# Patch stage of a vision tower: images loaded by channel into 112 partitions, half images in groups of 16, four result buffers

## The chip, the cores and the metric

The kernel runs on one core of one Trainium2 chip. The metric is the device time of one execution, in microseconds. Three executions of the kernel before gave 3536.22, 3531.46 and 3524.28 us, so the median is 3531.46 us.

## What is computed

64 images of 3 x 224 x 224 are cut into patches of 16 x 16 and turned into 64 x 196 tokens of 192 numbers; an attention layer and a feed-forward layer with a mixture of four experts follow. Only the first part bears on the change:

```python
B, c, H, Wd = features.shape            # 64, 3, 224, 224
h, w = (H // P1, Wd // P2)              # 14 x 14 patches
x = features.reshape(B, c, h, P1, w, P2)
x = jnp.transpose(x, (0, 2, 4, 3, 5, 1))
x = x.reshape(B, h * w, P1 * P2 * c)    # 768 numbers a patch
x = _layernorm(x, ln1_g, ln1_b)
x = jnp.einsum('bnd,de->bne', x, W) + b # 768 -> 192
x = _layernorm(x, ln2_g, ln2_b)
```

Everything after it (two attention phases named a and b, and the feed-forward phase f) reads these tokens from device memory and is the same in both kernels.

## The kernel before

The program runs four phases one after the other: tokenize_phase, attention_phase twice, ffn_phase. At the end of each phase all engines meet, so the next phase starts when the slowest engine of the phase is done; SP waits there for its last stores. All tiles of the patch stage bear the prefix t_ in the profile.

**Tiling.** A group is 8 whole images. One row of patches of one image is one partition, so a group fills 8 x 14 = 112 partitions (R), and each partition holds 3 channels x 3584 numbers (16 pixel lines of 224), in t_rows. There are two such buffers. A group is worked off in 7 units (UPG) of two patch columns each, so 8 groups make 56 units (NU). A unit u goes through four steps, each on several engines:

- A: DVE takes statistics of the two columns (L1036, L1043), POOL makes of them a scale and a shift (L27, L29, L952, L954);
- B: ACT applies these (t_xn, L990), PE transposes the result (L1082), ACT rounds it to 16 bits (t_xh, L995), DVE takes the rest (t_xl, L1049);
- C: PE multiplies with the weights in three passes (t_yp, L776; 38 matmuls a unit with the bias), DVE takes the statistics of the result (L1056, L1060), POOL makes scale and shift (L27, L29, L967, L969);
- D: ACT applies them (t_yn, L1005), POOL multiplies and adds the second affine pair (L958, L960), SP stores the tokens (L921).

**Order.** Each engine runs the same function `step` for s = -2 ... 56, and in step s it works on A of unit s+2, B of s+1, C of s and D of s-1. An engine executes what its step lists in that order and stops at each semaphore that isn't there yet. POOL's step lists A, D, C. The middle steps are a loop in the program (Fori, L869) of 14 steps a round; the first steps and the last ones are written out.

**Loads and stores.** SP issues all of them, in one queue. The next group's 8 images are loaded one by one, 588 KB each, two images in each of the first four units of a group, into the buffer that the group before has left (L903). A unit's tokens are stored as 112 rows of 384 numbers, 168 KB (L921). In SP's step the two loads stand ahead of the store. t_yn has two buffers: ACT may write unit u into its buffer when the store of unit u-2 has landed, and SP waits with the store of unit u-1 until the one before has landed:

```python
wait(act, out_s, 16 * (u - 1))          # ACT, ahead of L1005
waits(sp, (aff, 2 * (s - 1) + 2), (out_s, 16 * (s - 1)))   # SP, ahead of L921
```

At the start SP first issues 21 small loads (weights, L893; gains and offsets, L896; rows that are copied to all partitions, L898), and then the first group's 8 images.

Of the kernel before, what the change touches and what calls it, by code (L numbers as in the profile page):

```python
# [779 lines left out]
def tokenize_phase(nc, img, dst, ln1_g, ln1_b, w, bias, ln2_g, ln2_b):  # L780
# [19 lines left out]
    with ExitStack() as ctx:  # L800
        def sb(label, shape, dt):
            return ctx.enter_context(nc.sbuf_tensor(f"t_{label}", shape, dt))
# [41 lines left out]
        eps2 = sb("eps2", [R, 2], F32)  # L844
        yn = [sb(f"yn{i}", [R, 2, dim], F32) for i in range(2)]

# [3 lines left out]
        consts, w_in, w_ok, bp_s = sem("consts"), sem("w_in"), sem("w_ok"), sem("bp_s")  # L850
        rows_in = sem("rows_in")
# [3 lines left out]
        aff, out_s = sem("aff"), sem("out_s")  # L855

        LAG = {"A": 2, "B": 1, "C": 0, "D": -1}
        BODY = 2 * UPG

        def steps(eng, body):  # L860

            def kinds(s):
                return {k for k, lag in LAG.items() if 0 <= s + lag < NU}
            first = 3
            n = (NU - 2 - first) // BODY
            for s in range(-2, first):
                body(s, s, 0, kinds(s))
            if n > 0:
                with eng.Fori(0, n) as i:  # L869
                    for c in range(first, first + BODY):  # L870
                        body(BODY * i + c, c, i, set(LAG))
            for s in range(first + BODY * max(n, 0), NU + 1):
                body(s, s, 0, kinds(s))

        def group(c, i, lag):

            g, v = divmod(c + lag, UPG)
            return 2 * i + g, g % 2, v

# [3 lines left out]

        out_rows = dst.rearrange("(r x) d -> r x d", x=cols)
        block = ctx.enter_context(nc.Block())

        @block.sync
        def _(sp):
            w_view = w.rearrange("(q c) e -> c q e", c=chans)
            per = feats // chans // 128  # L890
            for k in range(KT):
                c, q = divmod(k, per)
                sp.dma_start(wraw[:, k, :], w_view[c, q * 128:(q + 1) * 128, :]).then_inc(w_in, 16)  # L893
                for col, vec in ((gcol, ln1_g), (bcol, ln1_b)):
                    v = vec.rearrange("(q c) -> c q", c=chans)[c, q * 128:(q + 1) * 128].rearrange("(p o) -> p o", o=1)
                    sp.dma_start(col[:, k:k + 1], v, allow_slow_non_contiguous=True).then_inc(w_in, 16)  # L896
# [27 lines left out]
            steps(sp, step)  # L924
            sp.wait_ge(out_s, 16 * NU)

        @block.gpsimd
        def _(pool):
# [15 lines left out]

            def step(s, c, i, kinds):
                if "A" in kinds:
                    u, b = s + 2, c % 2
# [7 lines left out]
                if "D" in kinds:  # L955
                    u, b = s - 1, (c - 1) % 2
                    wait(pool, yn_s, 2 * (u + 1))
                    pool.tensor_tensor(yn[b][:], yn[b][:], g2[:].unsqueeze(1).to_broadcast([R, 2, dim]), ALU.mult).then_inc(aff, 1)  # L958
                    wait(pool, aff, 2 * u + 1)
                    pool.tensor_tensor(yn[b][:], yn[b][:], b2[:].unsqueeze(1).to_broadcast([R, 2, dim]), ALU.add).then_inc(aff, 1)  # L960
                if "C" in kinds:
                    u, b = s, c % 2
# [8 lines left out]
            steps(pool, step)  # L971

        @block.scalar
        def _(act):
            act.wait_ge(w_in, 16 * (3 * KT + 3))
            act.mul(g16[:], gcol[:], WSCALE).then_inc(w_ok, 1)
# [5 lines left out]

            def step(s, c, i, kinds):
                if "B" in kinds:
                    u, b = s + 1, (c + 1) % 2
                    _, gb, v = group(c, i, 1)
                    for t in range(2):
# [9 lines left out]
                if "D" in kinds:  # L997
                    normalise(s - 1, (c - 1) % 2)

            def normalise(u, b):  # L1000

                wait(act, sh2_s, 2 * (u + 1))
                wait(act, out_s, 16 * (u - 1))
                for t in range(2):
                    act.activation(yn[b][:, t, :], yp[b][0:R, t * dim:(t + 1) * dim], ACT.Identity,  # L1005
                                   scale=rstd2[b][:, t:t + 1], bias=shift2[b][:, t:t + 1]).then_inc(yn_s, 1)

            steps(act, step)

        @block.vector  # L1010
        def _(dve):
# [14 lines left out]

            def step(s, c, i, kinds):
                if "A" in kinds:
                    u, b = s + 2, c % 2
                    g, gb, v = group(c, i, 2)  # L1030
                    wait(dve, rows_in, 16 * G_IMG * (g + 1))
                    wait(dve, mv_s, 2 * u)
# [4 lines left out]
                if "A" in kinds:  # L1037
                    u, b = s + 2, c % 2
                    wait(dve, sh_s, 2 * (u - 1))
# [4 lines left out]
                if "B" in kinds:  # L1044
                    u, b = s + 1, (c + 1) % 2
                    for t in range(2):
# [4 lines left out]
                if "C" in kinds:  # L1051
                    u, b = s, c % 2
                    wait(dve, yp_s, u + 1)
# [7 lines left out]

            steps(dve, step)

        @block.tensor
        def _(pe):
# [7 lines left out]

            def step(s, c, i, kinds):
                if "B" in kinds:
# [8 lines left out]
                if "C" in kinds:  # L1084
                    u, b = s, c % 2
                    for t in range(2):
# [7 lines left out]

            steps(pe, step)

# [919 lines left out]
```

## Time and profile before

| what | us |
|---|---|
| median of the three runs | 3531.46 |
| the profiled execution, its own time | 3541.15 |
| its span in the trace | 3539.1 |
| patch stage: from the start to the first instruction of the next phase | 523.84 |
| first instruction on an image's data | 63.39 |

The profiled execution is 9.7 us above the median and 2.05 us longer than its span. PE is busy for 84% of the whole span, DVE for 68%, ACT for 52%, POOL for 42%; in the patch stage the shares are lower. A row of the profile names the line, the engine, the operation and the tiles. In brackets stands the idle time of the engine ahead of it and what ended that time. SPq is SP's queue of transfers. The DMA share is the mean busy share of the core's 16 DMA engines.

### The profile page before, as it was taken

How to read it: one execution, taken by the hardware profiler on the slowest of the kernel's cores; microseconds unless marked ns; L12 is line 12 of the kernel's file. 1: busy time of each engine (PE TensorE's matmuls, PEld its weight loads, DVE VectorE, ACT ScalarE, POOL GpSimd, SP SyncE). 2: the span in 40 equal slices, each digit the busy share in tenths (PEclk: the TensorE clock that was granted, in tenths of full speed). 3: DMA queues.
4: the chain of work that ended last, by engine and by line, in shares of the span. 5: the costliest groups of instructions: out<-in, count | busy, mean ns of one | idle time of the engine just before them, and what ended most of it. 6: DMA issues, size and time to landing. Idle time of an engine off the chain costs nothing. (4 is left out here: it accounts for less than half of the span.)

```text
span 3539.1 us, 96114 instructions
## 1 busy us (share of the span) xinstructions
PE 2979.8 (84%) x31553; PEld 2278.1 (64%) x31553; DVE 2417.1 (68%) x5681; ACT 1849.0 (52%) x3603; POOL 1487.5 (42%) x2221
## 2 busy tenths in 40 slices
PE   2676766999999994899999997689987599999998
PEld 2666654556556652455556554678886488888887
DVE  2564656788888863788888884565555577777776
ACT  2454553666666661566666664556654244444443
POOL 1555562233333313344444431246666444444444
PEclk9887886999999996799999998899998799999999
DMA  7777733555555542465666653444433344444443
GB/s 93 103 105 100 106 59 89 133 140 148 145 138 143 141 123 68 121 157 149 154 154 160 156 150 91 124 117 131 124 120 103 92 66 66 66 65 66 66 66 50
DMA packets 503782, 393.69 MB, mean 111 GB/s; under 512 B 219818, under 2 KB 485068, under 8 KB 500812
## 3 DMA queue, kind: packets, MB, share of 16 engines
q1 hardware_dynamic: 465004, 343.59, 42.6%
q0 software_dynamic: 38496, 46.38, 7.5%
q8 instruction: 172, 2.82, 0.4%
q14 instruction: 110, 0.90, 0.1%
HBM read 232.59 MB, written 155.42 MB: 110 GB/s over the span
## 5 line engine op out<-in xcount | busy, mean ns | idle before, releaser
L1455 POOL DMA_INDIRECT out_dram<-f_yo,f_idg x202 | 331.5, 1641 | 426.7 <-DVE f_yo L1789 393.2
L566 DVE TENSOR_REDUCE b_mx<-b_mxp 98x4 f32<-98x784 f32 x384 | 371.5, 967 | 142.0 <-PE b_mxp L705 137.5
L566 DVE TENSOR_REDUCE a_mx<-a_mxp 98x4 f32<-98x784 f32 x384 | 371.5, 967 | 135.4 <-PE a_mxp L705 131.0
L1529 ACT ACTIVATE f_hf<-f_bank,f_b1c 128x256 f32<-128x256 f32 x606 | 254.3, 473 | 236.4 <-PE f_bank L776 236.3
L465 ACT ACTIVATE b_pt<-b_st 98x784 f32<-98x784 f32 x384 | 315.1, 821 | 61.0 <-PE b_st L691 57.5
L465 ACT ACTIVATE a_pt<-a_st 98x784 f32<-98x784 f32 x384 | 315.1, 821 | 58.7 <-PE a_st L691 55.4
L1945 PE MATMUL f_bank<-f_w2h,f_hh 128*128 x1212 | 299.7, 247 | 23.9 <-DVE f_hl L1773 23.4
L1946 PE MATMUL f_bank<-f_w2h,f_hl 128*128 x1212 | 298.2, 246 | 0.0
L1947 PE MATMUL f_bank<-f_w2l,f_hh 128*128 x1212 | 298.2, 246 | 0.0
L1082 PE MATMUL t_turned<-t_ident,t_xn 112*128 112x112 f32 x672 | 104.9, 313 | 179.0 <-ACT t_xn L990 174.3
L776 PE MATMUL f_bank<-f_el,f_w1h 128*128 128x256 f16 x1212 | 232.4, 274 | 0.0
L421 POOL TENSOR_TENSOR a_cn<-a_ctxs,a_rec 128x392 f32<-128x392 f32 x96 | 95.3, 1021 | 316.4 <-DMA a_rec<-a_recip 316.4
L1576 DVE TENSOR_TENSOR f_hl<-f_hf,f_hh 128x512 f16<-128x512 f32 x147 | 100.9, 686 | 184.9 <-ACT f_hf L1486 182.8
L1428 POOL DMA_INDIRECT f_listed<-f_xr,f_idx x196 | 200.7, 1024 | 57.1 <-issue 54.3
L1773 DVE TENSOR_TENSOR f_hl<-f_hf,f_hh 128x512 f16<-128x512 f32 x303 | 209.9, 693 | 10.4
L1082 PEld LDWEIGHTS t_turned<-t_ident,t_xn 112*128 112x128 f32 x672 | 84.3, 169 | 195.2 <-ACT t_xn L990 138.2
L766 PE MATMUL b_pr<-b_pf,b_cn 128*98 128x192 f32 x768 | 190.3, 359 | 23.1 <-DVE b_xo L613 16.0
L421 POOL TENSOR_TENSOR b_cn<-b_ctxs,b_rec 128x392 f32<-128x392 f32 x96 | 95.3, 1022 | 267.9 <-DMA b_rec<-b_recip 267.9
L766 PE MATMUL a_pr<-a_pf,a_cn 128*98 128x192 f32 x768 | 187.1, 354 | 23.6 <-DVE a_xo L613 16.0
L1521 ACT ACTIVATE f_xf<-f_bank,f_bcol,f_gcol 128x256 f32<-128x256 f32 x202 | 103.2, 561 | 179.5 <-PE f_bank L1915 179.5
L776 PE MATMUL t_yp<-t_wh,t_xh 128*112 128x192 f16 x672 | 182.6, 272 | 0.0
L776 PE MATMUL t_yp<-t_wl,t_xh 128*112 128x192 f16 x672 | 181.3, 270 | 0.0
(372 smaller groups left out, 9263.4 us busy)
## 6 DMA issues: line engine op xcount, KB each, us to landing
t_rows<-in_x_dram SPq DMA_DIRECT2D x64, 588.0 KB
f_xg<-f_listed SPq DMA_DIRECT2D x101, 264.0 KB, 2.8
a_qk<-a_qkh SPq DMA_DIRECT2D x128, 147.0 KB, 2.9
a_rec<-a_recip SPq DMA_DIRECT2D x128, 147.0 KB, 3.4
b_qk<-b_qkh SPq DMA_DIRECT2D x128, 147.0 KB, 2.8
b_rec<-b_recip SPq DMA_DIRECT2D x128, 147.0 KB, 3.5
a_qst<-a_qk SPq DMA_DIRECT2D x128, 110.2 KB, 3.0
a_kst<-a_qk SPq DMA_DIRECT2D x128, 110.2 KB, 3.1
```

The costliest lines, as they stand in the source:

```text
L421: pool.tensor_tensor(cn[b][:, g, :], ctxs[b][:, g, :], rec[:, g, :], ALU.mult).then_inc(cn_s, 1)
L465: act.activation(pt[k % PT][:].rearrange("p j a t -> p j (a t)"), st_ps[0:half_t, :, 0:unit_t], ACT.Exp, scale=sm_scale).then_inc(exp_s, 1)
L566: dve.tensor_reduce(mx[:, a, :, 2 * p:2 * p + 2].rearrange("p q j -> p j q"), mx_ps[0:half_t, :, 0:unit_t].rearrange("p j (q t) -> p j q t ...
L766: ins = pe.matmul(pr_ps[0:half_t, 0:dim], cn[b][:, g, x * half_t:(x + 1) * half_t], pf[:, g, :], start=(g == 0), stop=(g == 2))
L776: ins = pe.matmul(out, lhs, rhs, start=(i == 0), stop=(i == len(terms) - 1))
L1428: pool.indirect_dma_start(listed, bass.IndirectOffsetOnAxis(ap=idx[b % 2][:, 2 * (u - first_unit[b]) + t, c:c + 1], axis=0), xr[:, 2 * (u ...
L1455: pool.indirect_dma_start(out, bass.IndirectOffsetOnAxis(ap=idg[i % 3][:, t:t + 1], axis=0), yo[i % 3][:, t, :], None, compute_op=ALU.add) ...
L1529: act.activation(hf[pair][:, c % 2, :], p1[q % 2][:, (c % 2) * T:(c % 2) * T + T], ACT.Gelu, bias=b1c[:, bass.ds(e, 1), c], scale=1.0 / WS ...
L1773: dve.tensor_tensor(hl[i % 2][:, cs, :], hf[pair][:], hh[i % 2][:, cs, :], ALU.subtract).then_inc(ehl_s, 1)
L1945: pe.matmul(o, hh[i % 2][:, j, ts], high, start=(j == 0), stop=False)
L1946: pe.matmul(o, hl[i % 2][:, j, ts], high, start=False, stop=False)
L1947: pe.matmul(o, hh[i % 2][:, j, ts], low, start=False, stop=False)
```

## The change

Only the patch stage is changed.

1. A group is half of 16 images: 7 patch rows of each, again 112 partitions, 7 units and 56 units in all. The two halves of the same 16 images follow each other.
2. The load of a group is three transfers (N_LOADS), one for each channel, each into all 112 partitions, 14,336 bytes in each. One is issued in each of the first three units of a group. The two t_rows buffers have a semaphore each.
3. The first group's three loads are issued by ACT, at its very start, not by SP behind the weights.
4. The gains and offsets come in 6 transfers, not 12, so SP issues 15 small loads at the start, not 21.
5. t_yn has four buffers with a semaphore each. ACT waits for the store of unit u-4, and SP no longer waits for a store ahead of a store.
6. On SP, the store of a step stands ahead of the load. On POOL, the step lists A, C, D.
7. The loop is gone: all steps are written out on every engine.

```diff
-    G_IMG = 8
-    R = G_IMG * cols
-    n_groups = n_img // G_IMG
+    G_IMG = 16
+    G_ROWS = cols // 2
+    R = G_IMG * G_ROWS
+    n_groups = 2 * n_img // G_IMG
+    PARTS = 1
+    N_LOADS = chans * PARTS
+    YN = 4
...
-        yn = [sb(f"yn{i}", [R, 2, dim], F32) for i in range(2)]
+        yn = [sb(f"yn{i}", [R, 2, dim], F32) for i in range(YN)]
...
+        def load(eng, g, which):
+            c, part = divmod(which, PARTS)
+            src = img[g // 2 * G_IMG:(g // 2 + 1) * G_IMG, c].rearrange("i (h l) x -> i h l x", l=patch)
+            src = src[:, g % 2 * G_ROWS:(g % 2 + 1) * G_ROWS, part * lines:(part + 1) * lines].rearrange("i h l x -> i h (l x)")
+            to = rows[g % 2][:, c, part * lines * side:(part + 1) * lines * side]
+            eng.dma_start(to, src).then_inc(rows_in[g % 2], 16)
...
-            def load(g, b, images):
-                for j in images:
-                    src = img[bass.ds(g * G_IMG + j, 1)].rearrange("o c (h l) x -> (o h) c (l x)", l=patch)
-                    sp.dma_start(rows[b][j * cols:(j + 1) * cols], src).then_inc(rows_in, 16)
-
-            def step(s, c, i, kinds):
+            def step(s, kinds):
+                if "D" in kinds:
+                    u = s - 1
+                    g, v = divmod(u, UPG)
+                    wait(sp, aff, 2 * (u + 1))
+                    to = out_rows[g // 2 * G_IMG:(g // 2 + 1) * G_IMG, g % 2 * G_ROWS:(g % 2 + 1) * G_ROWS, 2 * v:2 * v + 2]
+                    sp.dma_start(to.rearrange("i h x d -> i h (x d)"),
+                                 yn[u % YN][:].rearrange("r x d -> r (x d)")).then_inc(out_s[u % YN], 16)
                 if "B" in kinds:
-                    g, gb, v = group(c, i, 1)
-                    if v < G_IMG // 2 and not (isinstance(g, int) and g + 1 >= n_groups):
+                    u = s + 1
+                    g, v = divmod(u, UPG)
+                    if v < 3 and g + 1 < n_groups:
                         if v == 0:
-                            waits(sp,
-                                  (xn_s, 2 * (s + 1)),
-                                  (st_s, 4 * (s + 1) + 1))
-                        else:
-                            wait(sp, xn_s, 2 * (s + 1))
-                        load(g + 1, 1 - gb, (2 * v, 2 * v + 1))
-                if "D" in kinds:
-                    g, gb, v = group(c, i, -1)
-                    waits(sp,
-                          (aff, 2 * (s - 1) + 2),
-                          (out_s, 16 * (s - 1)))
-                    sp.dma_start(out_rows[bass.ds(g * R, R), 2 * v:2 * v + 2, :], yn[(c - 1) % 2][:]).then_inc(out_s, 16)
-
-            load(0, 0, range(G_IMG))
+                            wait(sp, xn_s, 2 * u)
+                            wait(sp, st_s, 4 * u)
+                        for which in range(v * N_LOADS // 3, (v + 1) * N_LOADS // 3):
+                            load(sp, g + 1, which)
...
         def _(act):
-            act.wait_ge(w_in, 16 * (3 * KT + 3))
+            for which in range(N_LOADS):
+                load(act, 0, which)
+            act.wait_ge(w_in, 16 * (KT + 2 * chans + 3))
...
                 wait(act, sh2_s, 2 * (u + 1))
-                wait(act, out_s, 16 * (u - 1))
+                wait(act, out_s[u % YN], 16 * (u // YN))
```

**POOL, two units in the middle of the stage.** t_rstd and t_shift are step A's, the ones with _0 and _1 step C's, t_yn is step D's. Before:

```order
L27 TENSOR_TENSOR t_rstd<-t_mv,t_eps 112x2 [waits t_xn_s,t_mv_s]
L29 TENSOR_TENSOR t_rstd<-t_rstd,t_minus_half 112x2 [waits t_rsqrt_s]
L952 TENSOR_TENSOR t_shift<-t_mv,t_rstd 112x2 [waits t_rsqrt_s]
L954 TENSOR_TENSOR t_shift<-t_shift,t_minus_one 112x2 [waits t_sh_s]
L958 TENSOR_TENSOR t_yn<-t_yn,t_g 112x384 [waits t_yn_s]
L960 TENSOR_TENSOR t_yn<-t_yn,t_b 112x384 [waits t_aff]
L27 TENSOR_TENSOR t_rstd_0<-t_mv_0,t_eps 112x2 [waits t_yn_s,t_mv2_s]
L29 TENSOR_TENSOR t_rstd_0<-t_rstd_0,t_minus_half 112x2 [waits t_rsqrt2_s]
L967 TENSOR_TENSOR t_shift_0<-t_mv_0,t_rstd_0 112x2 [waits t_rsqrt2_s]
L969 TENSOR_TENSOR t_shift_0<-t_shift_0,t_minus_one 112x2 [waits t_sh2_s]
```

The two long operations on t_yn stand between A and C. In the changed kernel, in the same place:

```order
L27 TENSOR_TENSOR t_rstd<-t_mv,t_eps 112x2 [waits t_xn_s,t_mv_s]
L29 TENSOR_TENSOR t_rstd<-t_rstd,t_minus_half 112x2 [waits t_rsqrt_s]
L944 TENSOR_TENSOR t_shift<-t_mv,t_rstd 112x2 [waits t_rsqrt_s]
L946 TENSOR_TENSOR t_shift<-t_shift,t_minus_one 112x2 [waits t_sh_s]
L27 TENSOR_TENSOR t_rstd_0<-t_mv_0,t_eps 112x2 [waits t_yn_s,t_mv2_s]
L29 TENSOR_TENSOR t_rstd_0<-t_rstd_0,t_minus_half 112x2 [waits t_rsqrt2_s]
L953 TENSOR_TENSOR t_shift_0<-t_mv_0,t_rstd_0 112x2 [waits t_rsqrt2_s]
L955 TENSOR_TENSOR t_shift_0<-t_shift_0,t_minus_one 112x2 [waits t_sh2_s]
L959 TENSOR_TENSOR t_yn<-t_yn,t_g 112x384 [waits t_yn_s]
L961 TENSOR_TENSOR t_yn<-t_yn,t_b 112x384 [waits t_aff]
```

C now follows A directly, and the two operations on t_yn stand between C and the next unit's A.

**SP, around a group's first load.** Before (in the loop; the ISA rows hold waits on registers):

```order
L921 ISA [waits t_out_s,t_aff]
L921 DMA tokens<-t_yn 112x384
L39 ISA
L903 ISA [waits t_st_s,t_xn_s]
L903 DMA t_rows<-in_x_dram 14x3x3584
L903 ISA
L903 DMA t_rows<-in_x_dram 14x3x3584
```

In the changed kernel (x5 and the like: so many of the same in a row):

```order
L903 DMA tokens<-t_yn 16x7x384 [waits t_aff] x5
L879 DMA t_rows<-in_x_dram 112x1x3584 [waits t_st_s,t_xn_s]
L903 DMA tokens<-t_yn 16x7x384 [waits t_aff]
L879 DMA t_rows<-in_x_dram 112x1x3584
L903 DMA tokens<-t_yn 16x7x384 [waits t_aff]
L879 DMA t_rows<-in_x_dram 112x1x3584
L903 DMA tokens<-t_yn 16x7x384 [waits t_aff] x5
```

A store waits for POOL's result alone, and eight loads of 14 partitions have become three of 112.

**ACT, at the start of the program.** In the changed kernel the first group's loads stand ahead of all else there (before, ACT's first row is the one on t_g):

```order
L879 DMA t_rows<-in_x_dram 112x1x3584 x3
L970 ACT_TABLE_LOAD
L970 ACTIVATE t_g<-t_gcol 128x6 [waits t_w_in]
L974 ACTIVATE t_wf<-t_wraw,t_g 128x192 [waits t_consts,t_w_ok]
```

## Rows read from the trace of the kernel before

**Rows 1.** Waits between 161.7 and 219.9: engine, line, releaser, total, times, longest.

```profile
ACT t_yn L1005 <- DMA tokens<-t_yn: 28.0, 5, 6.8
POOL t_yn L958 <- ACT t_yn L1005: 19.8, 4, 6.7
```

**Rows 2.** SP's queue over one group, start and length in us.

```profile
161.68 18.91 SPq L921 DMA_DIRECT2D tokens<-t_yn  x4
...
208.34 0.35 SPq L921 DMA_DIRECT2D tokens<-t_yn  x1
208.98 0.84 SPq L903 DMA_DIRECT2D t_rows<-in_x_dram  x2
219.94 0.35 SPq L921 DMA_DIRECT2D tokens<-t_yn  x1
```

**Rows 3.** Stretches: PE, PEld, DVE, ACT, POOL busy, granted clock, DMA share, GB/s.

```profile
208.30:219.90 11.60, 7.42 (x50) 7.23 (x50) 3.97 (x12) 4.18 (x7) 4.53 (x10) 0.69 0.90 119
161.70:219.90 58.20, 40.25 (x350) 38.03 (x350) 32.62 (x100) 29.30 (x43) 31.54 (x70) 0.85 0.73 102
478.00:508.00 30.00, 25.41 (x267) 23.05 (x266) 24.12 (x78) 23.83 (x34) 25.52 (x57) 1.00 0.10 30
524.00:528.00 4.00, 0.00 (x0) 0.00 (x0) 3.29 (x2) 0.00 (x0) 1.39 (x9) 0.50 0.79 154
1904.00:1908.00 4.00, 3.77 (x43) 2.47 (x45) 2.45 (x4) 1.67 (x4) 0.00 (x0) 1.00 0.71 174
```

**Rows 4.** Start of the program, in order of time.

```profile
10.73 63.60 SPq L903 DMA_DIRECT2D t_rows<-in_x_dram  x14
15.55 0.21 ACT L976 ACTIVATE t_g<-t_gcol 128x6 f32<-128x6 f32 x1 [13.46 <-DMA t_b<-in_L_tok_ln_b_dram]
...
24.89 0.42 DVE L1024 SCALAR_TENSOR_TENSOR t_brow_parts<-t_brow_hi,t_row_mask,t_brow 112x192 f16<-112x192 f16 x1
63.39 1.94 DVE L1036 BATCH_NORM_STATS2 t_stats<-t_rows 112x6 f32<-112x384 f32 x4 [38.08 <-DMA t_rows<-in_x_dram]
```

**Rows 5.** Order of time without loads, one unit's path from 482.08.

```profile
482.08 0.20 POOL L27 TENSOR_TENSOR t_rstd<-t_mv,t_eps 112x2 f32<-112x2 f32 x1
...
483.64 1.95 ACT L990 ACTIVATE t_xn<-t_rows,t_shift,t_rstd 112x768 f32<-112x768 f32 x2 [0.56 <-POOL t_shift L954]
...
489.33 0.25 PE L776 MATMUL t_yp<-t_brow_parts,t_first_two 112*112 112x192 f16 x1
...
490.38 0.15 DVE L1060 BATCH_NORM_AGGREGATE t_mv<-t_stats 112x2 f32<-112x6 f32 x1
...
491.37 0.19 POOL L27 TENSOR_TENSOR t_rstd<-t_mv,t_eps 112x2 f32<-112x2 f32 x1
...
492.85 0.20 POOL L27 TENSOR_TENSOR t_rstd<-t_mv,t_eps 112x2 f32<-112x2 f32 x1
...
494.40 1.95 ACT L990 ACTIVATE t_xn<-t_rows,t_shift,t_rstd 112x768 f32<-112x768 f32 x2 [0.56 <-POOL t_shift L954]
```

**Rows 6.** PE in the first unit (slow clock) and later, in order of time.

```profile
74.98 0.37 PE L776 MATMUL t_yp<-t_wh,t_xh 128*112 128x192 f16 x1
...
75.14 0.37 PE L776 MATMUL t_yp<-t_wl,t_xh 128*112 128x192 f16 x1
...
80.62 0.25 PE L776 MATMUL t_yp<-t_wh,t_xh 128*112 128x192 f16 x1
...
80.71 0.25 PE L776 MATMUL t_yp<-t_wl,t_xh 128*112 128x192 f16 x1
```

**Rows 7.** First and last units on ACT and POOL, and the next phase's first instruction.

```profile
81.47 0.92 ACT L1005 ACTIVATE t_yn<-t_yp,t_shift,t_rstd 112x192 f32<-112x192 f32 x2 [0.63 <-POOL t_shift L969]
...
513.68 0.91 ACT L1005 ACTIVATE t_yn<-t_yp,t_shift,t_rstd 112x192 f32<-112x192 f32 x2 [4.07 <-DMA tokens<-t_yn]
518.25 0.91 ACT L1005 ACTIVATE t_yn<-t_yp,t_shift,t_rstd 112x192 f32<-112x192 f32 x2 [3.66 <-POOL t_shift L969]
...
523.84 0.74 POOL L364 MEMSET a_praw<- 96x768 f32 x1 [2.53 <-POOLq L800]
```

More of the change, by code:

```diff
@@ L850, in tokenize_phase @@
         consts, w_in, w_ok, bp_s = sem("consts"), sem("w_in"), sem("w_ok"), sem("bp_s")
-        rows_in = sem("rows_in")
+        rows_in = [sem(f"rows_in{i}") for i in range(2)]
         st_s, mv_s, rsqrt_s, sh_s = sem("st_s"), sem("mv_s"), sem("rsqrt_s"), sem("sh_s")
@@ L854, in tokenize_phase, with steps @@
         yp_s, sh2_s, st2_s, mv2_s, rsqrt2_s, yn_s = (sem("yp_s"), sem("sh2_s"), sem("st2_s"), sem("mv2_s"), sem("rsqrt2_s"), sem("yn_s"))
-        aff, out_s = sem("aff"), sem("out_s")
+        aff, out_s = sem("aff"), [sem(f"out_s{i}") for i in range(YN)]
         LAG = {"A": 2, "B": 1, "C": 0, "D": -1}
[L858 to L878, printed above, removed]
+        def steps(body):
+            for s in range(-2, NU + 1):
+                body(s, {k for k, lag in LAG.items() if 0 <= s + lag < NU})
         def patches(buf, col):
             return buf[:].rearrange("r c (l x) -> r (c l) x", l=patch)[:, :, col * patch:(col + 1) * patch]
-        out_rows = dst.rearrange("(r x) d -> r x d", x=cols)
+        out_rows = dst.rearrange("(i h x) d -> i h x d", h=cols, x=cols)
+        lines = patch // PARTS
+        def load(eng, g, which):
[4 more added lines that the diff above has]
+            eng.dma_start(to, src).then_inc(rows_in[g % 2], 16)
         block = ctx.enter_context(nc.Block())
@@ L893, in _ @@
                 sp.dma_start(wraw[:, k, :], w_view[c, q * 128:(q + 1) * 128, :]).then_inc(w_in, 16)
-                for col, vec in ((gcol, ln1_g), (bcol, ln1_b)):
-                    v = vec.rearrange("(q c) -> c q", c=chans)[c, q * 128:(q + 1) * 128].rearrange("(p o) -> p o", o=1)
-                    sp.dma_start(col[:, k:k + 1], v, allow_slow_non_contiguous=True).then_inc(w_in, 16)
+            for col, vec in ((gcol, ln1_g), (bcol, ln1_b)):
+                for c in range(chans):
+                    v = vec.rearrange("(q p c) -> c p q", c=chans, p=128)[c]
+                    sp.dma_start(col[:, c * per:(c + 1) * per], v, allow_slow_non_contiguous=True).then_inc(w_in, 16)
@@ L927, in _ @@
+                        for which in range(v * N_LOADS // 3, (v + 1) * N_LOADS // 3):
+                            load(sp, g + 1, which)
+            steps(step)
+            for i in range(YN):
+                sp.wait_ge(out_s[i], 16 * ((NU - i + YN - 1) // YN))
         @block.gpsimd
@@ L943, in _, with step @@
                                pattern=[[-1, 128]], channel_multiplier=1).then_inc(consts, 1)
-            def step(s, c, i, kinds):
+            def step(s, kinds):
                 if "A" in kinds:
-                    u, b = s + 2, c % 2
+                    u, b = s + 2, s % 2
                     wait(pool, mv_s, 2 * (u + 1))
@@ L969, in step @@
                     pool.tensor_tensor(shift2[b][:], shift2[b][:], minus_one[:], ALU.mult).then_inc(sh2_s, 1)
-            steps(pool, step)
+                if "D" in kinds:
+                    u, b = s - 1, (s - 1) % YN
+                    wait(pool, yn_s, 2 * (u + 1))
+                    pool.tensor_tensor(yn[b][:], yn[b][:], g2[:].unsqueeze(1).to_broadcast([R, 2, dim]), ALU.mult).then_inc(aff, 1)
+                    wait(pool, aff, 2 * u + 1)
+                    pool.tensor_tensor(yn[b][:], yn[b][:], b2[:].unsqueeze(1).to_broadcast([R, 2, dim]), ALU.add).then_inc(aff, 1)
+            steps(step)
         @block.scalar
         def _(act):
-            act.wait_ge(w_in, 16 * (3 * KT + 3))
+            for which in range(N_LOADS):
+                load(act, 0, which)
+            act.wait_ge(w_in, 16 * (KT + 2 * chans + 3))
             act.mul(g16[:], gcol[:], WSCALE).then_inc(w_ok, 1)
@@ L981, in _, with step @@
                 act.mul(bspread[:, k, :], ones[:], bcol[:, k:k + 1]).then_inc(w_ok, 1)
-            def step(s, c, i, kinds):
+            def step(s, kinds):
                 if "B" in kinds:
-                    u, b = s + 1, (c + 1) % 2
-                    _, gb, v = group(c, i, 1)
+                    u, b = s + 1, (s + 1) % 2
+                    g, v = divmod(u, UPG)
+                    gb = g % 2
                     for t in range(2):
@@ L1025, in _, with step @@
                                      op0=ALU.mult, op1=ALU.add).then_inc(bp_s, 1)
-            def step(s, c, i, kinds):
+            def step(s, kinds):
                 if "A" in kinds:
-                    u, b = s + 2, c % 2
-                    g, gb, v = group(c, i, 2)
-                    wait(dve, rows_in, 16 * G_IMG * (g + 1))
+                    u, b = s + 2, s % 2
+                    g, v = divmod(u, UPG)
+                    gb = g % 2
+                    wait(dve, rows_in[gb], 16 * N_LOADS * (g // 2 + 1))
                     wait(dve, mv_s, 2 * u)
@@ L1060, in step @@
                         dve.bn_aggr(mv2[b][:, t, :], stats2[:, t, :]).then_inc(mv2_s, 1)
-            steps(dve, step)
+            steps(step)
         @block.tensor
@@ L1072, in _, with step @@
             pe.wait_ge(w_ok, 3 + 2 * KT)
-            def step(s, c, i, kinds):
+            def step(s, kinds):
                 if "B" in kinds:
@@ L1084, in step @@
                 if "C" in kinds:
-                    u, b = s, c % 2
+                    u, b = s, s % 2
                     for t in range(2):
@@ L1093, in step @@
                     ins.then_inc(yp_s, 1)
-            steps(pe, step)
+            steps(step)
 def ffn_phase(nc, x3, h1, out, mlp, experts, ln_g, ln_b, gate_w, gate_b):
```

22 lines of the change are left out of this document (7 added, 15 removed).

## The prediction

> **What bounds the kernel now.** Only the patch stage changes, so I read the profile by stage: it ends at 523.84 us [rows 7], and what follows keeps its instructions and its time. In the stage three views matter. The waits over one group [rows 1] say who ends last: ACT waits 28.0 of 58.2 us for the store of the tokens before it may write t_yn, and POOL's 19.8 us of waiting for t_yn is the same wait passed on. SP's queue [rows 2] says why: four units without loads between their stores go by in 18.9 us, 6.3 us a step, while a unit whose two images were just queued takes 11.6 us (208.34 to 219.94). Two images are 2 x 602,112 bytes, so loads move at 1.204 MB / 11.6 us = 103.8 GB/s, and the store sits behind them in the queue; with the store's 172,032 bytes that makes the 119 GB/s of the stretch [rows 3]. So the images' transfer sets the step there, through the store and the two t_yn buffers. Second, the start: nothing touches an image before 63.39 us, because 8 images have to land first [rows 4]. Third, the order of time where no load is under way [rows 5] shows what is left if transfers are hidden: two units in 494.40 - 483.64 = 10.76 us, 5.38 us each.
>
> The DMA share tells how the loads are slow. It is 0.90 in that stretch, close to 14 engines of 16, and 119 GB/s over 0.90 x 16 engines is 8 GB/s for each busy engine. In 478 to 508, where nearly all traffic is stores from 112 partitions, 30 GB/s take a share of 0.10, or 300 GB/s at a full share; loads of weights into 96 and 128 partitions give 154 / 0.79 = 195 and 174 / 0.71 = 245 [rows 3]. An engine can do more than these loads get out of it.
>
> **Part 1, load rate (item 2).** A new load is 112 x 14,336 bytes = 1.606 MB. No row shows one of this shape. Bounds: 103.8 GB/s (15.5 us) from the loads it replaces, 300 GB/s (5.4 us) from the stores. I take 245 GB/s, 6.6 us, the value of the nearest full-width load. What does it have to meet? SP issues a group's first load behind the store of the unit u-2 (u is the group's first), that is when POOL begins A of unit u+2. The next group's first statistics must be done when POOL begins A of u+7: five steps, 30 us at the step found below, less 2.3 us for the statistics themselves. In it lie three loads, five stores at 172,032 B / 300 GB/s = 0.57 us, and some 2 us of latency: (30 - 2.3 - 2.9 - 2.1) / 3 = 7.6 us a load, 211 GB/s. At 245 the loads are hidden; at 195 (8.2 us) each of 7 groups waits 3 x 0.6 = 1.9 us, 13 us in all, which goes into the range.
>
> The Trainium skill ("SBUF — State Buffer", section on the DMA port swizzle) says that four adjacent partitions share one of 16 ports of some 27 GB/s. By that, 14 adjacent partitions have 4 on one port, 172 KB, an estimated 6.3 us or 95 GB/s an image, near the 5.8 us measured; and 112 partitions have at most 8 on a port, 115 KB, an estimated 4.2 us a load. The sum would be the same by it, since such a load is hidden as well.
>
> **Part 2, four t_yn buffers, no store behind store (item 5).** ACT now has two more steps for a store to land. A store behind one load is late by 6.6 us plus its own 2 or 3, far under the three steps it has; the 28.0 us go. I cost the rest at nothing, with the loads as cover as above.
>
> **Part 3, POOL's order (item 6).** Something else is late next. Take unit u's A on POOL, ended at 483.61 (1.53 us from 482.08), and follow [rows 5]: t_xn from 483.64, transposes, then the products of the unit before, the last at 489.33 + 0.25 = 489.58; its statistics are there at 490.53. Before, POOL is then still in D until 491.4, takes C (491.37 to 492.85, 1.5 us), and A of unit u+2 from 492.85 to 494.37. The loop spans two steps, 10.76 us. Three of POOL's pieces fill 482.08 to some 487.1, so D is 2.06 us. In the changed order C starts at once at 490.6, but D comes between C and that A: 483.61 to 490.6 is 7.0, + 1.5 + 2.06 + 1.5 = 12.06 us for two steps, **6.0 us a unit** against 5.38. POOL's own work is 5.1 us a unit, PE's 25.41 us of 30 at a step of 5.38, so 4.6 us; DVE 4.3, ACT 4.3 [rows 3]: none is the bound. The reorder is thus paid in this loop, 0.64 us a unit, though the step still falls from 8.3 (58.2 / 7).
>
> **Part 4, the start (items 3 and 4).** The statistics of unit 0 stand on DVE behind the work on the weights, which ended 9.8 us after the small loads were in (15.55 to 25.31) [rows 4]. The images come beside the weights now. If the weights are not disturbed: 25.3 us. If they land last of 4.82 + 0.84 MB at 245 GB/s: 0.8 + 23.1 + 9.8 = 34 us; at 195, 40 us. SP's queue is done six issues earlier. I take 30.
>
> **Part 5, the rest.** Written-out steps: nothing on the path; the last 13 units were written out before as well and include the 5.38 us stretch. From the first statistics to the first t_yn it took 81.47 - 63.39 = 18.1 us, kept. The last interval is 4.6 us (513.68 to 518.25). Behind the last t_yn came 5.6 us (518.25 to 523.84) [rows 7]; now D of unit 54 is still on POOL then, 1.1 more: 6.7.
>
> **Sum.** 30 + 18.1 + 54 x 6.0 + 4.6 + 6.7 = 383.4 us instead of 523.8, **140.4 us less**. 3541.15 - 140.4 = 3400.7 for a profiled execution; that lay 9.7 above the median, so **3391 us**, 4.0% less.
>
> **Rivals.**
>
> A. *POOL's order does not bind* (its pieces shift so that the old step holds): 54 x 0.62 = 33.5 us less, 3357. For it: POOL has idle time. Against it: the loop above has no slack in it.
>
> B. *The PE clock drops.* In the loaded group the granted clock was 0.85, in 478 to 508 it was 1.00 [rows 3]; a matmul starts every 0.16 us at the low level and every 0.08 at the high one [rows 6], so 38 of them cost 3.0 us more per loop, 1.5 us a unit if always slow (+81 us). At 0.85, some 0.3 of it: +24, 3415; half slow: +40, 3431. Against it: the long waits of PE, after which it was slow, go with the store waits, and the new step has gaps of about 1.4 us.
>
> C. *An engine gets no more out of a load than before* (slower). If what holds the loads is the rate of a DMA engine on rows of 14,336 bytes, then 16 engines instead of 14 give 103.8 x 16 / 14 = 118.6 GB/s, 13.5 us a load. Each group then takes 42 + 3 x (13.5 - 7.6) = 60 us; the start waits for 5.7 MB, about 55 us. 55 + 7 x 60 + 18.1 + 30 + 4.6 + 6.7 = 534 us, 10 more than before, and up to 25 more where the second group's loads share the start: some 3550 us. For it: the share of 0.90 means 14 busy engines. Against it: the rates of rows 3. It decides from about 120 GB/s down; above that the kernel is faster. The Trainium skill ("DMA: Bandwidth & Descriptors", section on the semaphore increment by 16) has a transfer run on the largest number of engines up to 16 that divides the slowest dimension of both sides: 14 before, which the trace agrees with, and 16 now.
>
> D. *A load does not spread at all*: its source has 16 images of 7 rows, its target 112 partitions. If it fell on 7 engines or fewer at the 300 / 16 = 19 GB/s of a store's engine, it would run at 130 GB/s or less: no gain, and with one engine a multiple of the stage.
>
> **How the numbers follow.** Forecast 0.74, A 0.08, B 0.08, C 0.07, D 0.03. The forecast's own range: start 25 to 40 (-5, +10), loads at 195 (+13), step 5.9 to 6.2 (-5, +11): 3380 to 3425. The range takes in A and B up to half slow and leaves out C and D: 3350 to 3440. A measurement can tell 0.3% (11 us) from no change. Faster by more: 0.91; within: 0.03 (part of C and D); slower: 0.06.
>
> **What would show it.** Right: first statistics near 30 us; no wait of ACT for the store; DVE's waits for t_rows near nothing after the first; t_yn every 6.0 us; POOL's step A of u+2 starting straight behind D while its statistics are already there; a granted clock near 1.0; the stage over at 383. A DMA share near 1 with long DVE waits for t_rows would mean C; a step of 5.4 means A; a clock of 0.85 or less with a step of 6.5 or more means B. Wrong: a stage end under 345 or over 435 us.

## The result

The changed kernel took 3400.99 us at the median of four runs (3387.60 to 3413.05), the kernel before 3527.87 us in the runs beside it (3524.12 to 3536.22). The ratio is 0.9636, with a 95% interval of 0.9595 to 0.9678: 3.6% less time. 3391 us were forecast, in a range of 3350 to 3440. The profiled execution took 3402.21 us. Six later runs of the same code (below, e12) lay higher, at a median of 3424.60 us and a ratio of 0.9706 (0.966 to 0.9751), so the changed kernel scatters more than the one before (those six lie 46 us apart, eleven of the kernel before beside them 31 us).

### The profile page after: what moved, and what is told of

Its sections match the earlier page's. It is cut to its first block and busy times, and to the rows that moved or that the text cites. A ratio compares the mean times of both kernels' runs of the same rounds, so it can differ in the third digit from the quotient of the medians.

```text
span 3400.3 us, 95327 instructions
## 1 busy us (share of the span) xinstructions
PE 2948.0 (87%) x31553; PEld 2234.3 (66%) x31553; DVE 2409.6 (71%) x5681; ACT 1847.6 (54%) x3603; POOL 1485.2 (44%) x2221
## 3 DMA queue, kind: packets, MB, share of 16 engines
q10 hardware_dynamic: 384, 4.82, 0.5%
## 5 line engine op out<-in xcount | busy, mean ns | idle before, releaser
L720 PE MATMUL b_pv<-b_pt,b_vp 98*32 98x196 f32 x3072 | 172.2, 342 | 0.2 <-ACT b_mrow L492 0.2
L720 PE MATMUL a_pv<-a_pt,a_vp 98*32 98x196 f32 x3072 | 169.8, 339 | 0.1
L776 PE MATMUL f_bank<-f_eh,f_w1h 128*128 128x256 f16 x606 | 165.6, 273 | 3.5 <-DVE f_el L1759 3.5
L776 PE MATMUL t_yp<-t_wh,t_xh 128*112 128x192 f16 x672 | 166.3, 247 | 0.0
```

The lines of the kernel that those rows point to most:

```text
L720: ins = pe.matmul(pv_ps[32 * h4:32 * h4 + 32, 0:tok], vp[b][:, 2 * a + kt, h, :], pt[(first + h4) // 2 % PT][:, h4 % 2, kt, :], start=(kt ...
L776: ins = pe.matmul(out, lhs, rhs, start=(i == 0), stop=(i == len(terms) - 1))
```

## The profile after

The span of the profiled execution, and the end of the stage on SP's queue (start, length): the last run of stores, then the next phase's first load.

```profile
span 3400.3 us, 95327 instructions
```

```profile
321.85 66.23 SPq L903 DMA_DIRECT2D tokens<-t_yn  x13
390.51 0.36 SPq L250 DMA_DIRECT2D a_wraw<-in_L_attn_w_qkv_dram  x1
```

The stage now ends at 390.5 us, 133.3 us earlier than the 523.84 of [rows 7]. The spans differ by 138.8; the other 5.5 us lie behind the stage, where both kernels have the same instructions. That part took 3015.3 us before and 3009.8 after, and between 2990 and 3020 us in all the profiles of this case, so I count it as scatter.

The longest of the waits between 60 and 330 us (engine and line, who released it, total us, times, longest us), which answer to [rows 1]:

```profile
PEld t_turned L1078 <- ACT t_xn L985: 74.8, 89, 1.6
ACT t_xn L985 <- POOL t_shift L946: 74.0, 45, 1.9
DVE t_stats L1052 <- PE t_yp L776: 60.3, 45, 1.5
PE t_turned L1078 <- ACT t_xn L985: 51.0, 44, 1.4
POOL t_rstd L27 <- DVE t_mv L1056: 43.4, 44, 1.2
ACT t_xh L990 <- PE t_turned L1078: 9.0, 45, 0.2
```

No DMA stands among them, nor among the shorter ones: ACT waits for no store and DVE for no image. What is left is one ring of short waits, a unit at a time: POOL for DVE's statistics of the product, ACT for POOL, PE for ACT, DVE for PE. It is the loop that the forecast named.

Stretches of the trace (busy us and instructions of PE, PEld, DVE, ACT, POOL, then granted clock, DMA share, GB/s), which answer to [rows 3]:

```profile
136.00:152.00 16.00, 12.35 (x130) 11.13 (x129) 11.99 (x41) 11.49 (x16) 11.35 (x28) 1.00 0.99 258
61.00:374.00 313.00, 246.15 (x2603) 225.05 (x2602) 231.53 (x725) 216.80 (x313) 233.25 (x521) 1.00 0.47 128
```

While a group's three loads run one behind the other, the engines move 258 GB/s at a share of 0.99, where 119 GB/s at 0.90 stood before, and over 313 us the granted clock stays at 1.00.

The step, on ACT and POOL (start, length, in brackets the idle time before it), which answers to [rows 5]:

```profile
205.23 1.00 POOL L959 TENSOR_TENSOR t_yn<-t_yn,t_g 112x384 f32<-112x384 f32 x1
206.31 1.00 POOL L961 TENSOR_TENSOR t_yn<-t_yn,t_b 112x384 f32<-112x384 f32 x1
207.26 0.20 POOL L27 TENSOR_TENSOR t_rstd<-t_mv,t_eps 112x2 f32<-112x2 f32 x1
...
208.83 1.95 ACT L985 ACTIVATE t_xn<-t_rows,t_shift,t_rstd 112x768 f32<-112x768 f32 x2 [1.46 <-POOL t_shift L946]
...
220.86 1.95 ACT L985 ACTIVATE t_xn<-t_rows,t_shift,t_rstd 112x768 f32<-112x768 f32 x2 [1.45 <-POOL t_shift L946]
```

POOL starts A at 207.26, straight behind the two operations of D, while its statistics were ready at 205.9 (DVE, L1039). Two units take 220.86 - 208.83 = 12.03 us, 6.0 us each.

The start, which answers to [rows 4]:

```profile
0.81 2.03 ACTq L879 DMA_DIRECT2D t_rows<-in_x_dram  x3
...
5.73 12.93 SPq L893 DMA_DIRECT2D t_bcol<-in_L_tok_ln_b_dram  x3
...
27.79 0.21 ACT L970 ACTIVATE t_g<-t_gcol 128x6 f32<-128x6 f32 x1 [23.64 <-DMA t_b<-in_L_tok_ln_b_dram]
...
37.12 1.93 DVE L1032 BATCH_NORM_STATS2 t_stats<-t_rows 112x6 f32<-112x384 f32 x4
```

The first statistics come at 37.12 us instead of 63.39, and they wait for the work on the weights and no longer for an image.

## Experiments

Each kernel is the changed one with the edit named. Ratios are to the kernel before, run beside it.

### What brings the gain: the loads or the buffers

**e2: the old loads, four buffers.**

```diff
-    G_IMG = 16
-    G_ROWS = cols // 2
+    G_IMG = 8
+    G_ROWS = cols
...
-    N_LOADS = chans * PARTS
+    N_LOADS = G_IMG
...
+            j = g * G_IMG + which
+            src = img[j:j + 1].rearrange("o c (h l) x -> (o h) c (l x)", l=patch)
+            to = rows[g % 2][which * cols:(which + 1) * cols]
...
-                    if v < 3 and g + 1 < n_groups:
+                    if v < 4 and g + 1 < n_groups:
```

Two images are issued in each of a group's first four units, and the store's rows follow the new groups.

> The changed kernel with the old loads alone: groups of 8 whole images, one load of 14 partitions for each image, two in each of the first four units; four t_yn buffers, no store waiting for a store, and all else as changed. Theory (the rate of the loads is what counts; the store waits were only where it showed): a group needs 4.82 MB at 104 GB/s = 46.4 us in a window of 27.7 us, so it takes 42 + 24 = 66 us, DVE waits for t_rows some 24 us a group, ACT for no store, and the time is some 3590 us, 1.017 of before. Rival (the store waits were the cause, and four buffers cure them with slow loads too): steps of 6 us, near 3420 us.

Measured: 3582.40 us, ratio 1.0166 (1.0129 to 1.0203). DVE's waits between 60 and 330 us, the first statistics of two groups in a row, and between them the issue of the second group's first images:

```profile
DVE t_stats L1031 <- DMA t_rows<-in_x_dram: 78.4, 4, 22.9
```

```profile
117.84 1.94 DVE L1031 BATCH_NORM_STATS2 t_stats<-t_rows 112x6 f32<-112x384 f32 x4 [11.91 <-DMA t_rows<-in_x_dram]
...
134.91 0.79 SPq L878 DMA_DIRECT2D t_rows<-in_x_dram  x2
...
184.71 1.94 DVE L1031 BATCH_NORM_STATS2 t_stats<-t_rows 112x6 f32<-112x384 f32 x4 [21.98 <-DMA t_rows<-in_x_dram]
```

A group takes 184.71 - 117.84 = 66.9 us and the next 64.9, against the 66 worked out, and no wait of ACT for a store is left. The theory holds: the wait that stood on top before, ACT for the store, can be removed altogether, and the kernel becomes slower, because the images still come slowly (4.82 MB in the 49.8 us from 134.91 to 184.71, 97 GB/s) and DVE waits for them instead. It is slower than the kernel before because the rest of the change costs something where loads are slow. In the kernel before, SP issued the next group's first images 9.2 us behind a group's first statistics (114.27 and 123.42 us in its trace), here 17.1 us behind them (117.84 and 134.91). These 8 us are what a group takes more than the 58.2 us of before. The likely reasons are the new order on SP, where the load now stands behind the store, and the new order on POOL, which makes that store later; no run tests them.

**e4: the old loads, two buffers** (e2 with `YN = 2`).

> The changed kernel with the old loads (8 images of 14 partitions a group) and two t_yn buffers, the rest as changed. The kernel with the old loads and four buffers took 3582 us. Theory (with slow loads the buffers don't matter either: a group waits for its images, and a store wait only falls into that wait): 3580 to 3600 us. Rival (four buffers were worth something with slow loads): over 3620 us.

Measured: 3584.40 us, ratio 1.0148 (1.0113 to 1.0183). ACT's wait for the store is back, and DVE's wait for images is smaller, 50.7 us in place of 78.4, in the same 270 us:

```profile
ACT t_yn L999 <- DMA tokens<-t_yn: 76.8, 13, 7.3
DVE t_stats L1031 <- DMA t_rows<-in_x_dram: 50.7, 4, 12.9
```

3582 and 3584 us: with slow loads the number of buffers makes no difference that this can measure. ACT's 76.8 us of waits cost nothing, because a group ends with its images either way.

**e3: the new loads, two buffers** (`YN = 2`).

> The changed kernel with two t_yn buffers, nothing else. Theory (with fast loads the buffers matter little): a store lands 2.5 us after issue and 7.1 behind a load; with two buffers ACT is held up to 2.3 us three times a group, of which 1.5 us are slack, so 0 to 20 us more than the changed kernel: 3400 to 3420 us, 0.964 to 0.970 of before. Rival (the buffers are an equal part of the gain): ACT waits for stores as before, over 60 us more, over 0.98 of before.

Measured: 3424.50 us (3397.24 to 3438.04), ratio 0.970 (0.9639 to 0.9762), just above what the theory gave. But the trace does not show the mechanism that I expected. Between 60 and 330 us ACT waited once for a store, in the 17th of its steps:

```profile
ACT t_yn L1000 <- DMA tokens<-t_yn: 1.3, 1, 1.3
```

```profile
164.72 0.91 ACT L1000 ACTIVATE t_yn<-t_yp,t_shift,t_rstd 112x192 f32<-112x192 f32 x2 [1.28 <-DMA tokens<-t_yn]
```

Yet the stage ended at 434.33 us, 43.8 later than with four buffers, and the step was 6.83 us from the third unit to the end. A row of PE, a stretch of two steps and one of 50 us (columns as in [rows 3], the granted clock third from the end):

```profile
209.65 1.72 PE L1078 MATMUL t_turned<-t_ident,t_xn 112*128 112x112 f32 x12 [2.86 <-ACT t_xn L985]
```

```profile
204.00:206.00 2.00, 2.00 (x27) 2.00 (x26) 1.87 (x7) 1.36 (x3) 1.83 (x4) 1.00 0.99 301
206.00:208.00 2.00, 0.79 (x10) 0.59 (x8) 1.96 (x8) 0.00 (x0) 1.84 (x3) 1.00 0.57 159
208.00:210.00 2.00, 0.35 (x4) 0.35 (x5) 1.86 (x6) 1.43 (x2) 1.62 (x7) 1.00 0.52 136
210.00:212.00 2.00, 1.88 (x18) 1.67 (x17) 1.00 (x4) 1.80 (x3) 1.92 (x4) 0.84 0.99 251
212.00:214.00 2.00, 2.00 (x15) 2.00 (x14) 0.95 (x2) 1.39 (x4) 1.28 (x5) 0.50 0.95 258
...
100.00:150.00 50.00, 40.59 (x377) 39.16 (x378) 31.76 (x99) 31.77 (x46) 31.41 (x72) 0.86 0.52 141
```

Two steps run close together, then PE waits 2.86 us for ACT, and about 2 us after it has started again its clock stands at 0.50 (1.2 GHz) for some 3 us. A matmul then starts every 0.16 us, not every 0.08, the products are late, and with them the next pair of steps: the pattern makes the gap that keeps it alive. In the changed kernel, with four buffers, PE's two gaps were 1.35 and 0.97 us and the clock stayed at 1.00.

How it began stands 100 us ahead of the only wait for a store:

```profile
59.30 1.71 PE L1078 MATMUL t_turned<-t_ident,t_xn 112*128 112x112 f32 x12 [1.60 <-ACT t_xn L985]
```

```profile
60.00:62.00 2.00, 1.87 (x17) 1.78 (x17) 1.87 (x7) 1.80 (x4) 1.82 (x4) 0.80 0.00 0
62.00:64.00 2.00, 2.00 (x15) 2.00 (x14) 0.66 (x1) 0.58 (x2) 1.76 (x5) 0.50 0.07 20
```

PE had waited 1.60 us for ACT, not for a store, and some 2 us later the clock was at its low level. So nothing in this trace lays the slower rhythm to the two buffers; the expectations of e8 and e11 below, written with the wait of 1.3 us taken for its start, have this wrong. The median agrees: e3's ratio of 0.970 is that of six later runs of the changed kernel, 0.9706 (e12). The changed kernel's trace has the same gap in the same unit (1.61 us, ahead of 59.67) and no fall of the clock behind it. Nearly the same instructions thus have two rhythms, 6.0 and 6.8 us a step, and the question became what decides between them.

### The two rhythms

**e8: one disturbance.** DVE does eight more statistics ahead of unit 20, which took 3.7 us in the trace:

```diff
+                    if u == 20:
+                        for k in range(8):
+                            dve.bn_stats(extra[:, k, :], patches(rows[gb], 2 * v)[:, 0:half // patch, :])
```

> The changed kernel with one disturbance: DVE repeats a statistics instruction eight times, 4.3 us, ahead of its work on unit 20, into a tile nobody reads. With two buffers for t_yn one wait of 1.3 us near the start was followed by steps of 6.83 us and a granted clock of 0.87 for the whole stage, where the changed kernel has 6.0 and 1.0. Theory (the stage has two rhythms at the same work; a single hold-up puts it into the slower one, in which two steps bunch, PE pauses for 2.9 us, and its clock drops for some 3 us in every second step): steps of 6.8 us for all 35 units behind the disturbance, the stage 4 + 35 x 0.82 = 33 us longer, some 3430 us. Rival (two buffers for t_yn cost it, not the rhythm): steps of 6.0 us again after a few units, 4 us longer, some 3404 us.

Measured: 3441.61 us (3428.41 to 3447.41), ratio 0.9752 (0.9726 to 0.9779). The stretches before and behind the disturbance:

```profile
100.00:150.00 50.00, 39.78 (x426) 36.55 (x425) 37.06 (x114) 34.55 (x51) 37.50 (x84) 1.00 0.63 165
200.00:250.00 50.00, 38.03 (x360) 36.42 (x359) 34.75 (x109) 30.28 (x44) 34.59 (x78) 0.88 0.47 133
300.00:350.00 50.00, 39.06 (x359) 37.63 (x360) 31.82 (x98) 31.29 (x45) 31.67 (x73) 0.86 0.46 127
```

t_yn came every 5.8 and 6.2 us in turn before, and every 6.1 and 7.5 us in turn at 200 us and later. The stage ended at 421.27 us: 30.8 later than without the disturbance, of which 3.1 are a later start and 3.7 the disturbance, so 24 us are the rhythm. The theory is confirmed: 3.7 us at one place put the stage into the slower rhythm, and it stays there to the end, with four buffers.

**e9: the same disturbance, POOL's step in the old order A, D, C.**

> The same disturbance of 4.3 us at unit 20, in the kernel with POOL's old order A, D, C. That one had a step of 6.7 us at its third unit and then went back to 5.38. Theory (the slow rhythm needs the longer loop; with the order A, D, C the stage recovers): 3367 + 4 = 3371 us, the granted clock back at 1.0 within a few units. Rival (any order can stay slow): steps of 6 us or more to the end, 3390 us or more.

Measured: 3363.77 us, ratio 0.954 (0.9503 to 0.9578), no different from e1 below. In the stretch of the disturbance the clock fell, and it was back in the next:

```profile
150.00:200.00 50.00, 41.18 (x414) 38.68 (x412) 39.30 (x121) 33.90 (x49) 37.24 (x85) 0.93 0.43 125
200.00:250.00 50.00, 43.32 (x457) 39.52 (x456) 41.31 (x132) 39.70 (x56) 41.77 (x92) 1.00 0.52 145
```

t_yn came 9.2, 5.8, 5.7, 6.7, 5.8 us apart and then every 5.0 and 5.8 us again. With the shorter loop the stage leaves the slower rhythm. Two traces show the same without a disturbance. In e1 and e10, both with the order A, D, C, the clock fell to 0.50 behind the same gap of 1.6 us as in e3 (e1 at 62 us, e10 at 56); one step took 6.7 us, and then the step was back at 5.0 to 5.8. Of the eleven traces with the new loads, all with this gap in that unit, these three have a fall of the clock behind it.

**e11: old order A, D, C with two buffers.**

> POOL's old order A, D, C with two t_yn buffers. With the new order two buffers cost 24 us at the median (3424 against 3401), by my reading not through their waits (1.3 us in the trace) but because these put the stage into the slower rhythm. Theory: with the order A, D, C, which leaves that rhythm again, two buffers cost only the waits themselves: 3367 to 3385 us, steps of 5.4 to 5.7. Rival (two buffers cost it themselves): 3390 us or more.

Measured: 3366.46 us, ratio 0.9528 (0.9493 to 0.9563), against 3366.75 with four buffers. The trace has more store waits than e3 (nine between 60 and 330 us), and they cost nothing that can be measured; its stage ended at 359.25 us, e1's at 359.18:

```profile
ACT t_yn L1000 <- DMA tokens<-t_yn: 8.4, 9, 1.8
```

So four buffers in place of two are worth nothing here, and e3's slower rhythm was not their doing.

**e12: the changed kernel once more.**

> The changed kernel once more, to see how its times scatter. Theory (it can fall into the slower rhythm by chance, at any unit): times between 3388 and 3445 us, each with a mean granted clock that falls as the time rises, from 0.948 to about 0.93, while the kernel before and the one with the order A, D, C scatter less. Rival (it never falls into it): all within 3388 to 3413.

Measured: 3401.27, 3406.55, 3412.86, 3436.34, 3444.64 and 3447.57 us, with mean granted clocks of 0.945, 0.947, 0.943, 0.935, 0.934 and 0.931 over the whole execution. The trace belongs to the 3406.55 us run and has the faster rhythm throughout. The kernel before, run beside it, lay between 3518.64 and 3549.40 us with clocks of 0.923 to 0.936, and e11 between 3360.85 and 3375.35. The slower half of the six, at a lower clock and 30 to 45 us above, fits a stage that spent part of its time in the slower rhythm, and e3 shows that this can begin without any hold-up from outside; none of those runs left a trace, so this is likely and not shown.

### POOL's order

**e1: the order A, D, C again.**

```diff
                 if "A" in kinds:
...
+                if "D" in kinds:
+                    u, b = s - 1, (s - 1) % YN
...
                 if "C" in kinds:
...
-                if "D" in kinds:
-                    u, b = s - 1, (s - 1) % YN
```

> The changed kernel with POOL's step in the old order A, D, C. Theory (the new order puts D's 2.06 us into the two-step loop): the step falls from 6.02 to the old 5.38 us, the stage ends 54 x 0.64 = 34 us earlier, near 356 us in place of 390.5, the whole at 0.954 of before (some 3367 us). Rival (the order of POOL costs nothing, the 6.0 us come from elsewhere): step 6.0, 0.964 of before, as the changed kernel.

Measured: 3366.75 us (3356.45 to 3371.74), ratio 0.9543 (0.9507 to 0.9578). t_yn comes every 5.0 and 5.8 us in turn, 5.38 on average, and the next phase starts at 359.18 us, 31.3 earlier than in the changed kernel. The order on POOL in item 6 thus cost what the loop said, 33.5 us, less the one slow step and a start 0.6 us later.

### The kind of load

**e5: 14 engines, but 112 partitions.** Groups of 8 whole images, the partition being patch row x 8 + image; the store follows the same order:

```diff
+            src = img[g * G_IMG:(g + 1) * G_IMG, c].rearrange("i (h l) x -> h i (l x)", l=patch)
```

> The changed kernel with groups of 8 whole images, still three loads into 112 partitions, but the partition is patch row x 8 + image, so that the slowest dimension is 14, not 16. Theory (the target's spread over partitions sets the rate, not the number of engines): a DMA share of 0.87 while loads run, at 220 GB/s (14/16 of the 250 measured), loads still hidden, 3400 to 3415 us. Rival (what holds a load is the rate of an engine, or the count of 14): 104 GB/s as before, waits of DVE for t_rows of over 20 us a group, some 3590 us.

Measured: 3441.93 us, ratio 0.9751 (0.971 to 0.9792). The rate settles the question it was made for:

```profile
340.00:356.00 16.00, 11.52 (x107) 10.91 (x108) 11.19 (x36) 10.42 (x15) 10.95 (x26) 0.89 0.88 204
```

A share of 0.88 is 14 engines of 16, as with the old loads, but they move 204 GB/s, not 119. By engine in work that is 14.5 GB/s, against 8 with 14 adjacent partitions and 16 in the changed kernel. So the spread over partitions alone gives 85 of the 139 GB/s gained. Two more engines at 14.5 GB/s would bring it to an estimated 230; the rest, up to 258, these runs do not explain. The Trainium skill ("SBUF — State Buffer", on the DMA port swizzle) offers a reason for the first part by its map of partitions to ports; no run here shows the ports themselves. The time came out 27 us above what I expected, for two reasons that the trace shows: the start is later (first statistics at 45.90 us, the small loads being held up longer), and one wait of DVE for an image, 4.0 us at 131 us, was followed by the slower rhythm to the end, with steps of 6.8 us.

### The start

**e6: the first group's loads on SP, behind the small ones.**

```diff
-            for which in range(N_LOADS):
-                load(act, 0, which)
...
+            for which in range(N_LOADS):
+                load(sp, 0, which)
```

> The changed kernel with the first group's three loads issued by SP behind its small loads, not by ACT ahead of all; all else as changed. Theory (on ACT's queue the big rows of the images hold up the small loads, which landed at 27.8 us and not at 15.6, and the start waits for those): the small loads land near 12.5 us, the work on the weights ends near 22, the images land at about 8 + 4.82 MB / 250 GB/s + 2 = 29 to 31 us, so the first statistics come at 31 in place of 37.1, the whole 6 us less, some 3395 us. Rival (ACT's early start is worth more than the hold-up): first statistics after 38 us.

Measured: 3417.21 us (3389.89 to 3456.17; the median without the longest of the four is 3404.73), ratio 0.9678 (0.9636 to 0.972): by the total not better. The trace is of the run with 3389.89 us and has a stage end at 387.77 us. Its rows at the start:

```profile
13.46 0.21 ACT L971 ACTIVATE t_g<-t_gcol 128x6 f32<-128x6 f32 x1 [11.37 <-DMA t_b<-in_L_tok_ln_b_dram]
```

```profile
34.75 1.94 DVE L1033 BATCH_NORM_STATS2 t_stats<-t_rows 112x6 f32<-112x384 f32 x4 [11.54 <-DMA t_rows<-in_x_dram]
```

The hold-up is real: without the images ahead of them the small loads are in at 13.5 us, not at 27.8. But the images are in only at 34.75, so 2.4 of the 6 us come out. The spread of the times is the largest of all kernels here, with clocks from 0.956 down to 0.929 in step with it.

**e7: e6 with the order A, D, C.**

> The changed kernel with both: POOL's old order A, D, C and the first group's loads on SP behind the small ones. If the two add up: stage end at 359 - 6 = 353 us, some 3361 us, 0.9525 of before. If the start is absorbed later: as with POOL's order alone, 0.954.

Measured: 3356.18 us (3350.95 to 3375.93), ratio 0.9516 (0.949 to 0.9542), stage end 355.41 us. By the traces the two edits add up: alone they ended the stage 31.3 us (e1) and 2.7 us (e6) earlier, together 35.1. By the times, e7's interval overlaps that of e1.

**e10: e7, and SP holds the second group's loads until the first group's have landed.**

```diff
+                        if u == 0:
+                            sp.wait_ge(rows_in[0], 16 * N_LOADS)
```

> POOL's old order A, D, C, the first group's loads on SP behind the small ones, and in addition SP waits for the first group's images before it issues the second group's. Without that wait the first statistics came at 35.4 us, not at the 29 to 31 expected, with five loads of 1.6 MB in the queue together. Theory (a queue works at all of them, so the second group's rows delay the first's): first statistics at 8.1 + 4.82 MB / 250 GB/s + 2 = 29.4 us, the stage 6 us shorter than the 355.4, some 3350 us. Rival (the queue works in order and the rate at the start is lower): still 34 to 35 us.

Measured: 3366.05 us, ratio 0.9532 (0.9504 to 0.9561). The first statistics came at 32.05 us, 3.3 earlier than in e7, and the stage ended at 353.21, 2.2 earlier. So the second group's rows did hold up the first's, as the theory had it, by about half the 6 us; the rest is left open. In the total it can't be seen.

## Why the prediction was right

**Load rate.** Taken as 245 GB/s; 258 GB/s in the trace. The row I took it from was misread: what is issued between 1904 and 1908 us is no load of weights but loads of b_rec and stores of b_qk, 147 KB each. That its rate was so near is luck; it was not needed, since anything above the 211 GB/s of the window would have hidden the loads. The loads are hidden, as the window of 27.7 us said, and e2 shows the other side of the same arithmetic: 66 us a group from 104 GB/s, measured 66.9 and 64.9.

**Buffers.** I said that the 28.0 us of store waits go, and they went. But the forecast leaned on their being the place where slow loads showed, and the experiments show that more sharply than the text did: four buffers bring nothing by themselves, with slow loads (e2, e4) or with fast ones (e1, e11). Not tested by themselves were the store that no longer waits for a store, the store ahead of the load on SP, the fewer small loads and the written-out steps. The top line of the waits before named the store; the cause was what stood ahead of it in the queue.

**POOL's order.** The loop gave 12.06 us for two steps; the trace has 12.03. e1 took it back and gained 34 us at the median (3401 to 3367), 31.3 in the stage. Rival A, that the order does not bind, has fallen.

**The start.** This was the term mis-sized: 30 us taken, 37.1 measured. The small loads landed at 27.8 us, behind the images, and even later than my bound (24 us) for their landing last at 245 GB/s; SP could not even issue them, with one row of three issues standing for 12.9 us.

**Sum.** 37.1 to the first statistics, 19.2 to the first t_yn, 54 steps of 5.99 = 323.7, 3.5 for the last interval and 7.0 behind it make 390.5 us, where the forecast had 30 + 18.1 + 324 + 4.6 + 6.7 = 383.4. Of the 7.1 us between them the start makes 7.1, and the other terms cancel. For the profiled execution I had 3400.7 us, and it took 3402.21; that this is so near is in part luck, for the part behind the stage came out 5.5 us shorter and covered most of the start. The median, 3401 us, came out 10 us above the forecast of 3391, because I took off 9.7 us, by which the profiled execution of the kernel before lay above its median; here it lay 1.2 above.

**Rivals.** C (an engine gets no more out of a load) is refuted by the rate and by e5, and D (a load does not spread) by the DMA share of 0.99. B (a lower clock) gave way in the profiled run, but it was better than I took it for. I had tied the low clock to the long waits of PE for stores, and thought that gaps of 1.4 us were safe. In most traces they are, but behind a gap of 1.6 us the clock fell in three of eleven, and with this order of POOL one fall, or one hold-up, bunches two steps into one gap of 2.9 us, which then renews itself. The price was too low: for a clock of 0.85 I had +24 us, and e3, at 0.86 to 0.89, cost 43.8, because the bunched steps also wait. My +40 was for a stage half of whose matmuls are slow, so its nearness to 43.8 is chance. The chance of 0.08 was probably too low as well: half of e12's runs lie there by their times.

## What to carry to other kernels

A wait for a store in a shared queue may be a wait for the loads ahead of it: look at the rate and at the DMA share before adding buffers. A transfer into 14 adjacent partitions had 14 engines busy at 8 GB/s each, one into 112 partitions 14 engines at 14.5; load by the layout that fills the partitions, and let the order of the work follow. Once transfers are hidden, follow one unit round the engines and ask of each engine's program order which piece stands inside the loop: two operations of 1.0 us each moved out of it are worth 3367 us in place of 3401. That version with the start on SP as well (e7, 3356 us, 0.952 of before) has the lowest median here; it beats both kernels, though not clearly e1.

## What was not expected of the hardware

**A rhythm with its own clock.** The same instructions on the same data run at 6.0 us a step with a clock of 1.00, or at 6.8 with 0.86 to 0.89. A disturbance of 3.7 us moved the stage from the one to the other for the 35 units that were left, and so did, in e3, one fall of the clock behind a gap of 1.6 us. In the loop that is 1.3 us shorter for two steps the slower rhythm did not last (e1, e9, e10). Why the clock fell behind that gap in three traces and not in the other eight is left open.

**Small loads beside big rows.** Three loads of 1.6 MB on ACT's queue held up fifteen small ones on SP's: the weights' median time to landing was 19.1 us, against 2.2 when they went first (e6). The hold-up reached SP's issuing itself.

**The rest of the program.** With the same instructions it took 2990 to 3020 us in the profiles of this case, so a difference of 10 us in one execution's total says nothing; the end of the stage in the trace does.
